# An expert layer on one core: raw weights loaded into the place of their low part, four places, loads up to three experts ahead

## What is computed

```python
base = jnp.einsum('bsi,oi->bso', x, W_base)            # plus a rank-16 adapter chosen per sequence
h = x W_t; z = h A[adapter]; l = z B[adapter]; y = base + (l W_p) * scaling[adapter]
probs = softmax(y @ gate_w.T); topk_w, topk_idx = top_k(probs, 2)      # weights renormalised
g = einsum('th,eih->tei', y, w_gate); u = einsum('th,eih->tei', y, w_up)   # i = 352, h = 512
out = x + sum over the two chosen experts of  topk_w * (silu(g) * u) @ w_down.T
```

## Time and profile of the kernel before

| | |
|---|---|
| time, median of 3 runs | 343.33 us (343.33, 341.28, 343.49) |
| profiled execution | 341.91 us, of which span 340.1 us |
| granted TensorE clock, mean | 0.995 |
| PE, DVE, ACT, POOL busy | 329.9, 235.5, 180.0, 128.9 us |
| DMA | 82.47 MB, mean 243 GB/s |

### The profile page before, as it was taken

One profiled execution on the slowest core, in us unless ns is written; L12 is line 12 of the kernel. 1 busy time (PEld: TensorE's weight loads), 2 busy tenths in 40 slices (PEclk: granted clock), 3 DMA queues, 4 the chain that ended last, 5 costly groups with the idle time before them and its releaser, 6 DMA issues.

```text
span 340.1 us, 7756 instructions
## 1 busy us (share of the span) xinstructions
PE 329.9 (97%) x1847; PEld 290.7 (85%) x1847; DVE 235.5 (69%) x314; ACT 180.0 (53%) x246; POOL 128.9 (38%) x85
## 2 busy tenths in 40 slices
PE   7999999989999999999999999999999999999992
PEld 5657788879999999989988999989999989989981
DVE  3639799896646677584886948788586588779310
ACT  4368823623466444556646365485555476574321
POOL 0000000112634635556382653745645281534313
PEclk9999999999999999999999999999999999999997
DMA  7975887749599899999999997999979979931153
GB/s 270 411 290 238 308 331 254 268 154 324 169 347 290 182 271 263 296 216 271 246 263 288 324 345 183 286 307 300 314 179 268 248 210 275 308 42 26 17 74 44
DMA packets 47927, 82.47 MB, mean 243 GB/s; under 512 B 5552, under 2 KB 22576, under 8 KB 47792
## 3 DMA queue, kind: packets, MB, share of 16 engines
q1 hardware_dynamic: 38912, 62.96, 56.1%
q0 software_dynamic: 8960, 18.89, 25.4%
HBM read 60.59 MB, written 19.92 MB: 237 GB/s over the span
## 4 chain that ended last, share of the span: by engine, by line
PE 95%; DMA 1%; issue 1%; ACT 1%; POOLq 1%; DVE 0%; ACTq 0%
PE bank L707 46%; PE bank L736 24%; PE bank L681 4%; PE bank L455 4%; PE bank L492 3%; PE bank L571 3%; PE bank L572 3%; PE bank L573 3%; DMA lead_sb<-lead 1%; PE bank L581 1%; PE bank L609 1%; PE bank L624 1%; POOLq L96 0%; PE bank L529 0%; DVE hh L1201 0%
## 5 line engine op out<-in xcount | busy, mean ns | idle before, releaser
L1288 POOL DMA_INDIRECT out<-ys,sidx x40 | 79.9, 1997 | 115.8 <-DMA out<-ys,sidx 65.9
L362 DVE TENSOR_TENSOR w_lo<-w_raw,w_hi (+2 forms) x32 | 76.2, 2380 | 11.2 <-issue 9.3
L1267 POOL DMA_INDIRECT xg<-y_rows,gidx x40 | 48.5, 1212 | 91.7 <-issue 75.4
L707 PE MATMUL bank<-w_hi,xt_hi 128*128 x320 | 82.0, 333 | 1.1 <-ACT y_st L802 1.1
L707 PE MATMUL bank<-w_hi,xt_lo 128*128 x320 | 79.0, 323 | 0.0
L707 PE MATMUL bank<-w_lo,xt_hi 128*128 x320 | 78.9, 323 | 0.0
L360 ACT ACTIVATE w_hi<-w_raw (+2 forms) x32 | 64.7, 2021 | 9.5 <-DMA w_raw<-wall 5.6
L871 ACT ACTIVATE sg<-bank 128x352 f32<-128x352 f32 x40 | 18.5, 463 | 77.1 <-PE bank L707 70.0
L707 PEld LDWEIGHTS bank<-w_hi,xt_hi 128*128 128x128 f32 x320 | 54.7, 189 | 2.5 <-issue 1.7
L707 PEld LDWEIGHTS bank<-w_hi,xt_lo 128*128 128x128 f32 x320 | 56.1, 189 | 0.0
L707 PEld LDWEIGHTS bank<-w_lo,xt_hi 128*128 128x128 f32 x320 | 56.1, 188 | 0.0
(11 more groups left out here) (188 smaller groups left out, 363.3 us busy)
## 6 DMA issues: line engine op xcount, KB each, us to landing
w_raw<-wall SPq DMA_DIRECT2D x16, 1408.0 KB
w_raw<-wall SPq DMA_DIRECT2D x16, 768.0 KB
xs<-xg SPq DMA_DIRECT2D x132, 64.0 KB
y_rows<-y_st SPq DMA_DIRECT2D x16, 256.0 KB, 6.8
x_st<-xin SPq DMA_DIRECT2D x6, 512.0 KB, 13.5
lead_sb<-lead SPq DMA_DIRECT2D x4, 512.0 KB, 5.4
head_sb<-head SPq DMA_DIRECT2D x2, 640.0 KB, 8.8
wb_sb<-wb SPq DMA_DIRECT2D x2, 512.0 KB, 11.5
```

The source lines that it names most:

```text
L362: e.tensor_tensor(w_lo[:, bass.ds(dst, n)], raw, hi, ALU.subtract).then_inc(own, 1)
L707: mm = e.matmul(bank[2 + 2 * s + t % 2][:, 0:INTER], a, w[:, bass.ds(at + (k * GU + s * INTER), INTER)], start=k == 0 and i == 0, stop=k = ...
L1267: e.indirect_dma_start(out=xg[t % NXG][:], out_offset=None, in_=y_dram, in_offset=bass.IndirectOffsetOnAxis(ap=gidx[:, t:t + 1], axis=0)). ...
L1288: e.indirect_dma_start(out=out, out_offset=bass.IndirectOffsetOnAxis(ap=sidx[:, t:t + 1], axis=0), in_=ys[t % NYS][:], in_offset=None, bou ...
```

## The change

`w_raw` no longer has places of its own. It lies on the same bytes as `w_lo`, so the load of an expert writes where its low part will stand, and VectorE subtracts in place. The memory of the two raw places goes into a fourth place: four for `w_hi`, four for `w_raw`/`w_lo`. A run's place is its number modulo 4. `later_weights(t)`, at a run's first tile, now loads run+3 instead of run+2. The place that it loads into was that of run-1, so SP waits for TensorE to have finished the tile before t (`m_gu` ≥ t for `gu`, `m_dn` ≥ t for `dn`) instead of for VectorE's low part. Run 2 is loaded ahead of these (behind the gather of tile 3 and the end of the first stage), `N_SOON` is 3. ScalarE no longer waits for a free place before it writes `w_hi`. The routing's word for a tile loses its slot number, and with it four small VectorE instructions. The first stage's tiles are laid out anew (`x_hi`, `x_lo` in two pieces each); nothing is computed otherwise.

```diff
-NRAW, NSPLIT = 2, 3
+NSLOT = 4
-N_LEAD, N_COPY, N_SOON = 9, 5, 4
+N_LEAD, N_COPY, N_SOON = 9, 5, 3
...
-        w_hi = weights("w_hi", [P, NSPLIT * EW], F32R)
-        w_lo = weights("w_lo", [P, NSPLIT * EW], F32R)
-        w_raw = weights("w_raw", [P, NRAW * EW], F32)
+        w_hi = region(0, NSLOT * SLOT)("w_hi", [P, NSLOT * EW], F32R)
+        w_raw = region(o_lo[0], NSLOT * SLOT)("w_raw", [P, NSLOT * EW], F32)
+        w_lo = region(o_lo[0], NSLOT * SLOT)("w_lo", [P, NSLOT * EW], F32R)
...
                 if act:
-
                     e.wait_ge(d_w[part], (run + 1) * 16)
-                    if t < NSPLIT:
-                        e.wait_ge(m_tb, 2)
-                    else:
-                        e.wait_ge(m_gu if gu else m_dn, t - 2)
                 else:
                     e.wait_ge(a_gu if gu else a_dn, run + 1)
-                split_part(e, act, src + off, dst + off, n, own)
+                split_part(e, act, at + off, n, own)
...
-                run, new, at, _ = tile_word(e, t)
-                with e.If(new * SKIP + runs - run > SKIP + NRAW):
-                    ex = table(e, T_REX, bass.ds(run + NRAW, 1), 0, NEXP - 1)
+                run, new, _ = tile_word(e, t)
+                with e.If(new * SKIP + runs - run > SKIP + NSLOT - 1):
+                    ex = table(e, T_REX, bass.ds(run + NSLOT - 1, 1), 0, NEXP - 1)
+                    at = e.snap(((run + NSLOT - 1) & (NSLOT - 1)) * EW)
                     for part in PARTS:
-                        e.wait_ge(v_gu if part == "gu" else v_dn, run + 1)
+                        if t == 0:
+                            e.wait_ge(m_tb, 2)
+                        else:
+                            e.wait_ge(m_gu if part == "gu" else m_dn, t)
                         e.sem_inc(p_turn, 1)
-                        e.wait_ge(d_w[part], (run + NRAW) * 16)
+                        e.wait_ge(d_w[part], (run + NSLOT - 1) * 16)
                         e.sem_inc(p_turn, 1)
                         load_part(e, part, ex, at)
...
             e.wait_ge(d_g[N_LATE], 16)
+            e.wait_ge(m_y, CH)
+            for part in PARTS:
+                e.wait_ge(d_w[part], 32)
+                load_part(e, part, table(e, T_REX, 2, 0, NEXP - 1), 2 * EW)
             for t in range(N_SOON):
                 later_weights(t)
...
-                if N_SOON <= t - N_COPY < NTILE - NRAW:
+                if N_SOON <= t - N_COPY <= NTILE - NSLOT:
                     later_weights(t - N_COPY)
...
-            step(e.tensor_scalar(g2[:, 0, 0:5], rc[:, R_TH3:R_TH3 + 5], run, None, ALU.is_le))
-            step(e.tensor_reduce(third, g2[:, 0, 0:5], AX_X, ALU.add))
...
-            step(e.scalar_tensor_tensor(slot3, third, -float(NSPLIT), run, ALU.mult, ALU.add))
-            step(e.scalar_tensor_tensor(new, new, float(W_NEW), run, ALU.mult, ALU.add))
...
```

More of the change, by code:

```diff
@@ L118, in build @@
         SLOT = EW * 4
-        o_hi, o_lo, o_raw = 0, NSPLIT * SLOT, 2 * NSPLIT * SLOT
-        o_b = o_raw + NRAW * SLOT
+        o_hi = [i * SLOT for i in range(NSLOT)]
+        o_lo = [(NSLOT + i) * SLOT for i in range(NSLOT)]
+        o_b = 2 * NSLOT * SLOT
         B_SIZE = 36864
@@ L168, in build @@
         wd = r_t("wd", [P, 4, NEXP], F32)
-        wc = [r_t(f"wc{i}", [P, 1], F32) for i in range(4)]
+        wc = [r_t(f"wc{i}", [P, 1], F32) for i in range(2)]
         rr = r_t("rr", [P, 2], F32)
@@ L339, in split_weights @@
                     e.wait_ge(a_gu if gu else a_dn, 1)
-                    e.wait_ge(m_g, 1)
-                split_part(e, act, (NRAW - 1) * EW + off + first, off + first, n - first, own)
+                split_part(e, act, off + first, n - first, own)
                 return
-            run, new, src, dst = word
-            fresh = new > 0 if t < surely.get(e.engine, NFULL) else new * W_SLOT * 2 + count > W_SLOT * 2 + t
+            run, new, at = word
+            fresh = new > 0 if t < surely.get(e.engine, NFULL) else new * W_ANY + count > W_ANY + t
             with e.If(fresh):
@@ L348, in split_weights, with split_part @@
                     e.wait_ge(d_w[part], (run + 1) * 16)
-                    if t < NSPLIT:
-                        e.wait_ge(m_tb, 2)
-                    else:
-                        e.wait_ge(m_gu if gu else m_dn, t - 2)
                 else:
                     e.wait_ge(a_gu if gu else a_dn, run + 1)
-                split_part(e, act, src + off, dst + off, n, own)
-        def split_part(e, act, src, dst, n, own):
-            raw, hi = w_raw[:, bass.ds(src, n)], w_hi[:, bass.ds(dst, n)]
+                split_part(e, act, at + off, n, own)
+        def split_part(e, act, at, n, own):
+            raw, hi, lo = [v[:, bass.ds(at, n)] for v in (w_raw, w_hi, w_lo)]
             if act:
@@ L404, in _ @@
                         e.wait_ge(d_w[part], 16)
-                        load_part(e, part, table(e, T_REX, 1, 0, NEXP - 1), 0)
+                        load_part(e, part, table(e, T_REX, 1, 0, NEXP - 1), EW)
                 if c == C_LOAD:
@@ L1071, in _ @@
             has, g2, ce = wd[:, 0], wd[:, 1:3], wd[:, 3]
-            new, third, slot3, of16 = (v[:] for v in wc)
+            new, of16 = (v[:] for v in wc)
             run, before = rr[:, 0:1], rr[:, 1:2]
@@ L1163, in _ @@
             half = PARTS["gu"][1] // 2
-            raw_0 = (NRAW - 1) * EW
             e.wait_ge(a_gu, 1)
-            e.wait_ge(m_g, 1)
-            e.tensor_tensor(w_lo[:, 0:half], w_raw[:, raw_0:raw_0 + half], w_hi[:, 0:half], ALU.subtract).then_inc(v_chain, 1)
+            e.tensor_tensor(w_lo[:, 0:half], w_raw[:, 0:half], w_hi[:, 0:half], ALU.subtract).then_inc(v_chain, 1)
             done[0] += 1
@@ L1279, in scatter @@
                     if t >= NYS + N_FREE:
-                        first = table(e, T_WORD, t, 0, W_SLOT * NSPLIT - 1) & W_NEW
+                        first = table(e, T_WORD, t, 0, 2 * W_NEW - 1) & W_NEW
                         done = {u: e.snap(first + 16 * (u // NYS)) for u in late}
```

65 lines of the change are left out of this document (30 added, 35 removed).

## The result

The changed kernel's median is 348.25 us (345.75, 346.65, 349.86, 350.11); beside it the kernel before ran at 343.41 (341.28, 343.33, 343.49, 350.57). The ratio is 1.0153, with a 95% interval of 1.0113 to 1.0193: slower by 1.5%. The 350.57 us is a run of a slower state that some executions fall in, and the ratio leaves it out. A second set of runs gave 1.0145 (1.0101 to 1.0188). The forecast was 345.9, range 342.0 to 349.3. The profiled execution is the fastest of the four: 345.75 us, span 343.8, against 341.91 and 340.1 before.

The account below looks back on a forecast made before the run. The prediction took TensorE, busy 329.9 of 340.1 us, as the bound. A gain of 0.7 us and a cost of 4.0 us gave +3.3 on a base of 342.6: 345.9 us, range 342.0 to 349.3.

Parts of the forecast that it names:

- The place and the chain: Run 4's load ahead of tile 9's rows on SP; 4 us of other engines between gate_up(7) and gate_up(8).
- The prediction's mechanism: On SP's queue, rows behind a load do not overtake it, so tile 9's rows land late and TensorE waits.
- The landing: Tile 9's rows behind run 4's load, issued at 114.7, were taken to land at 126.0.
- the cost term: At tile 9's rows: x_turned(9) may begin at 122.0 without harm, so rows at 126.0 cost 4.0 us.
- The 10.2 us read off the kernel before: Time from issue to landing of run 4's load in the kernel before, read from tile 11's row packets (9.2 to 11.2).
- The far bound of 15.7 us: Slowest load found, run 7's: tile 9's rows would land at 130.4, a cost of 8.4 us.
- The deadline and the price of lateness: VectorE's x_turned(9) may begin at 122.0 without harm; each later us costs one.
- The gain: Tile 16 to 17: loads one run further ahead end ScalarE's wait for run 7's weights; 0.73 us back, taken as -0.7.
- Edits at nothing: Subtraction in place, four removed routing instructions and ScalarE's dropped waits were each counted as 0 us.
- In time anyway: Rival: tile 9's rows land by 122.0, from 341 GB/s up; only the gain is left, 341.9 us; chance 0.12.
- The second stall: Rival: tile 11's rows, behind two loads, land at about 142.7, 2.2 us past the limit; 348.1 us; chance 0.15.
- The sum: Whole kernel: -0.7 + 4.0 = +3.3 us, giving 345.2 on the profiled execution and 345.9 from the base of 342.6.

Follow-up runs that it names:

- Run 4: Not a follow-up: a run of tiles within the kernel; its weight load was issued at 121.31 us in the kernel before, 114.26 in the changed kernel.
- the last run above: Changed kernel with loads two tiles later on SP's queue (N_COPY 7, run 4's load behind tile 10's rows), measured again: 341.12 us, ratio to the kernel before 0.9947.
- run 5: Not a follow-up: a run of tiles within the kernel; the changed kernel loads its weights by later_weights(5), behind tile 10's rows on SP's queue.
- run 7: Not a follow-up: a run of tiles within the kernel; its gu was issued at 170.40 us in the kernel before, 158.48 in the changed kernel.
- old kernel with the load ahead: Kernel before, with run 4's load moved behind tile 8's rows instead of tile 10's: 350.76 us, ratio 1.0229.
- gu alone: Changed kernel with only run 4's gu ahead of tile 9's rows and its dn directly behind them: 345.24 us, ratio to the kernel before 1.0046.
- dn behind tile 10: Changed kernel with run 4's gu ahead of tile 9's rows and its dn behind tile 10's rows: 345.80 us, ratio to the kernel before 1.0090.
- busy gap: Changed kernel with 24 extra matmuls on TensorE ahead of its wait for ht_lo(6): 349.01 us, ratio to the kernel before 1.0142.
- the layout alone: Changed kernel's layout (four places, subtraction in place) with the old lead, loading run+2 at the old queue positions: 342.07 us, ratio to the kernel before 0.9970.

## Why the prediction was right in kind, and where its sizes failed

**The place and the chain: right.** Run 4's load at 114.26 (forecast 114.7), rows behind it from 115.48 (116.3), `x_turned(9)` late after an idle time ended by `xs<-xg`, other engines in the chain between `gate_up(7)` and `gate_up(8)`, a gain at tile 17, and no other stall. The runs with the load one and two tiles later, and with the same place in the old kernel, show that this place and nothing else of the change makes the loss. The prediction's mechanism holds; a term of its sum was mis-sized.

**The landing: the step that failed.** The prediction took tile 9's rows as landed at 126.0, 11.3 us after the issue; it was 128.83, 14.6 us, and 15.7 in two further traces. This is the cost term, 4.0 us in the sum, that was too small: it measured 5.85 and 6.71. Three parts of its working were too favourable. The 10.2 us read off the kernel before came from where most row packets had moved; `x_turned(11)` ran there only at 133.85, so up to 12.5 us were open, and the last packets, not most of them, set the landing. In the last run above, with the load in its old place, VectorE did wait for tile 11's rows, which were usable 14.35 us after the load's issue at 121.44:

```profile
135.79 1.17 DVE L1178 STREAM_TRANSPOSE xt<-xs 128x512 f32<-128x512 f32 x1 [1.21 <-DMA xs<-xg]
```

The second part is the bytes. They were taken as 3.63 MB; the same view of the changed kernel from 114.3 to 128.8 us shows more, at a lower rate:

```profile
DMA packets 2611, 4.22 MB, mean 291 GB/s; under 512 B 233, under 2 KB 1263, under 8 KB 2610
...
q1 hardware_dynamic: 2199, 3.07, 74.7%
q0 software_dynamic: 411, 1.13, 27.4%
```

GpSimd's 1.13 MB were foreseen. Not counted were tile 10's rows, another 0.26 MB issued right behind tile 9's, and the first packets of run 5's load: 3.07 MB on q1 instead of 2.49. 4.22 MB at 291 GB/s are the 14.5 us measured, but only because both are read from that same stretch. By the forecast's own 298 to 326 GB/s, 4.22 MB give 12.9 to 14.2 us in place of 11.1 to 12.2. Run 5's packets, too, stand behind the rows on the queue; that they moved is no proof that they held the rows up. The third part is the rate of the rows themselves: where mostly row packets moved, the engines moved 240 GB/s against 340 just before, and the prediction priced the rows at the load's rate. In the changed kernel it shows in the last 2.8 us: from 126 to 128.8, 640 - 80 = 560 packets between 512 B and 2 KB still moved, at 221 GB/s:

```profile
DMA packets 761, 0.62 MB, mean 221 GB/s; under 512 B 80, under 2 KB 640, under 8 KB 761
```

One tile has 512 of them, so they are of both tiles. Whether bytes behind the rows, and not only ahead of them, hold them up is not settled: the step from dn right behind tile 9's rows to dn behind tile 10's points that way by 1.2 us, within the spread. The forecast by bytes for the second of them missed by 2 to 3 us again, so bytes over a rate give the earliest landing, and what the rest of it waits for stays open. The far bound of 15.7 us, taken from run 7, was the better guide.

**The deadline and the price of lateness: right.** The prediction said 122.0, 0.25 after the start of `gate_up(7)`, and one us for each us. In six traces (changed kernel twice, busy gap, old kernel with the load ahead, gu alone, dn behind tile 10) lateness was 6.41, 7.30, 7.48, 6.86, 5.58, 3.82 and the stall 5.85, 6.71, 6.83, 6.33, 4.83, 3.03: one for one, from a deadline 0.5 to 0.8 us behind the start of `gate_up(7)`, 0.3 to 0.5 later than forecast. A start of `x_turned(9)` at 126.0 would have cost 126.0 - 122.42 - 0.6 = 3.0 us in the first of them; the real start cost 5.85, and 6.7 in the second, against the 4.0 forecast.

**The gain: 0.9 instead of 0.7.** TensorE's step at tile 16 fell from 7.21 to 6.27. The 0.73 was read off the chain, whose piece of `gate_up(16)` starts at 178.75, 0.24 us behind the first matmul at 178.51. But the loss depends on the landing: with 11.35 us from issue to use it is there, with 9.9 us, in the layout alone, it is not.

**Edits at nothing: wrong by a little.** The subtraction in place did cost nothing (3.08 to 3.09 us). The dropped place number and waits probably did not save nothing: 0.6 us at tiles 31 to 36, present in every trace of the new layout, though these two edits were never run apart from it. I had looked at what ScalarE waits for, not at what it spends before an instruction. Two differences stay open. Behind the last scatter's start the span goes on for 4.7 to 5.0 us in the three traces of the old layout and for 3.8 to 4.1 in nine of the ten of the new, but for 5.2 in the tenth (busy gap). And in the new layout the last piece of `x_st` came late for ScalarE, by 0.95 to 1.36 us, in all four traces with an early full clock and in two of the other six; in the four, tile 0 stands 0.27 to 0.7 us later than in the kernel before:

```profile
29.09 1.07 ACT L782 ACTIVATE x_hi<-x_st 128x1024 fp32r<-128x1024 f32 x1 [1.22 <-DMA x_st<-xin]
```

In the three traces of the old layout that wait was 0, 0 and 0.34. Neither has been tested.

**The rivals.** "In time anyway" fell with the 4.22 MB at 291 GB/s, far from 341. The second stall did not come in the changed kernel: `x_turned(11)` ran at 140.4, near the limit of 140.5 that was forecast with a smaller delay, but by then TensorE was 6.5 us late itself. The run with dn behind tile 10's rows shows that the mechanism is real.

**The sum.** In the profiled execution: 0.7 at tile 0, + 5.85 at tile 8, - 0.94 at tile 17, - 0.65 from tile 31 to 36, - 0.9 behind the start of tile 39, - 0.3 in small steps, = 3.8 in span (3.7 by the rounded spans), where the forecast was 3.3. The near hit on that execution is chance in part: the cost was 1.8 too low, and unseen gains made up for most of it. In the medians, with the stall nearer the 6.71 of the second trace, the change costs 4.8 to 5.5 us.

## What to carry to other kernels

Before a large load is moved ahead on a queue, list what then stands behind it, work out for each the latest start that its reader can bear, and count every byte that the DMA engines will move until then on all queues, short packets at the lower rate that they show. What comes out is the earliest landing: here the real one was 2 to 4.5 us later, and it moved by 1 to 2 us between executions. Take the landing from when the reader really ran or from the last packet, never from when most packets had moved. A fourth place cost nothing; the queue position had to move back with it, by two tiles. For the gain at tile 17 alone an earlier issue in the old layout was enough. A second hardware queue brought the rows no sooner.

## What was not expected of the hardware

- Four DMAs, 256 KB of rows in all, issued on ScalarE's queue beside 2.2 MB on SP's, moved 1 packet in 4.5 us while SP's 2816-byte packets (rows of gu) were in flight, and went about one for one with it only beside the 2048-byte ones (232 to 270 packets in 4 us). The cause of the first 4.5 us was not tested.
- The same load and rows took 14.6, 15.7 and 15.7 us in three executions of nearly the same program and 13.5 in the old layout with the load ahead, a spread larger than the gain that the change was made of.
- After 4.04 us of idle time TensorE was granted half the clock (0.52 from 131.0 to 134.4), and it cost at most 0.1 us, since the work that it slowed was not what the next step waited for.
- Full clock was granted from 4.0 to 5.3 us after the start in six of the traces and from 8.9 to 9.8 us in seven, with TensorE's first matmul at 1.1 us in all. Within one layout tile 0 stands 0.9 to 2.2 us later in the second group; differences of single spans must be taken from tile 0 on.
